# Rope tables made on VectorE a round ahead, first queries turned inside the embedding stage, and a third buffer for x1

## What is computed

```
x = x + L0_ffn(L0_cond(x))          # 16 mixing matrices by sequence, then an int4 weight [512, 512] in fp16
x = x + L1_ffn(L1_cond(x))          # L1_cond: attention with a paged KV cache
x = x + L2_ffn(L2_cond(x))
x = x + L3_ffn(L3_cond(x))

L1_cond: q, k, v = x Wq, x Wk, x Wv     # 32 query heads, 8 key heads of 128
         q, k = rmsnorm(q) * wq, rmsnorm(k) * wk
         q, k = rope(q, pos), rope(k, pos)       # pos = length of the sequence's cache + token
         rope(t) = [t1 cos - t2 sin, t2 cos + t1 sin]
         keys = 512 cached ones (16 pages of 32) and the 32 new ones
         softmax(q keys^T * scale, masked by cache length) values, then Wo
```

## Time and profile before

| what | us |
|---|---|
| median of the three runs | 3247.13 |
| lowest and highest | 3244.84, 3252.37 |
| the profiled execution's own time | 3248.76 |
| its span, first to last instruction | 3246.8 |
| busy in the span: PE, DVE, ACT, POOL | 3034.6 (93%), 1556.9 (48%), 1293.1 (40%), 1532.6 (47%) |
| mean granted clock of TensorE | 0.976 of full |
| DMA | 378.26 MB, mean 117 GB/s |

### The profile page before, as it was taken

How to read it: one execution, slowest core, us unless ns; L and a number is a source line. 1 busy time by engine, 2 the same in 40 slices (tenths; PEclk the granted TensorE clock), 3 DMA queues, 4 the chain that set the end, 5 groups by cost and what they waited for, 6 DMA issues and landing times. The chain is left out here.

```text
span 3246.8 us, 55910 instructions
## 1 busy us (share of the span) xinstructions
PE 3034.6 (93%) x15256; PEld 2022.1 (62%) x15264; DVE 1556.9 (48%) x3931; ACT 1293.1 (40%) x3014; POOL 1532.6 (47%) x1323
## 2 busy tenths in 40 slices
PE   3799999999999999999999999999999986888887
PEld 2466666666666666666666666666666664555454
DVE  6544444444444444444444444444444444556555
ACT  1344444444444444444444444444444431222221
POOL 7355555555555555555555555555555520001000
PEclk9899999999999999999999999999999997999898
DMA  8544444434443444545444444344444443112110
GB/s 294 192 122 123 117 117 117 118 117 118 117 118 117 118 118 125 189 123 176 124 119 120 119 120 121 118 127 123 126 118 123 123 148 100 31 37 53 32 30 13
DMA packets 416196, 378.26 MB, mean 117 GB/s; under 512 B 83427, under 2 KB 347763, under 8 KB 414996
## 3 DMA queue, kind: packets, MB, share of 16 engines
q1 hardware_dynamic: 358484, 186.81, 20.2%
q0 software_dynamic: 50480, 174.40, 17.2%
q10 hardware_dynamic: 7056, 14.46, 1.2%
HBM read 341.23 MB, written 25.85 MB: 113 GB/s over the span
## 5 line engine op out<-in xcount | busy, mean ns | idle before, releaser
L533 DVE CUSTOM_DVE_ANT_0 ps_s<-ps_s,mask 128x544 f32<-128x544 f32 x512 | 374.9, 732 | 938.8 <-PE ps_s L360 929.2
L262 POOL DMA_INDIRECT v_sb<-in_v_rows_w,v_row x504 | 488.3, 969 | 469.3 <-PE ps_oT L385 258.7
L319 PE MATMUL ps_t<-wqkv,xT 128*128 128x512 f32 x1488 | 704.1, 596 | 0.0
L383 PEld LDWEIGHTS ps_oT<-pT,v_sb 128*128 128x128 f32 x4096 | 527.0, 192 | 186.6 <-issue 186.1
L433 ACT ACTIVATE ps_s<-ps_s,nmax 128x544 f32<-128x544 f32 x512 | 352.3, 688 | 628.9 <-DVE nmax L533 627.8
L383 PE MATMUL ps_oT<-pT,v_sb 128*128 128x128 f32 x4096 | 541.3, 275 | 9.8 <-issue 9.8
L343 PE MATMUL ps_t<-wo,oT 128*128 128x512 f32 x1024 | 524.8, 597 | 2.5 <-ACT oT L448 0.9
L359 PE MATMUL ps_s<-k_sb,qT 128*128 128x416 f32 x1024 | 446.9, 518 | 19.2 <-issue 15.2
L543 DVE TENSOR_SCALAR p_sb<-ps_s,rinv 128x544 f32<-128x544 f32 x512 | 401.3, 784 | 23.9 <-DVE rinv L540 0.3
L448 ACT ACTIVATE oT<-ps_oT 128x128 f32<-128x128 f32 x512 | 141.9, 277 | 637.0 <-PE ps_oT L385 634.3
L368 PEld LDWEIGHTS ps_pT<-ident_sb,p_sb 128*128 128x128 f32 x2048 | 251.3, 141 | 188.3 <-issue 185.4
(11 more groups left out here) (216 smaller groups left out, 3775.4 us busy)
## 6 DMA issues: line engine op xcount, KB each, us to landing
k_sb<-in_kT SPq DMA_DIRECT2D x2048, 64.0 KB
v_sb<-in_v_rows_w,v_row POOLq DMA_INDIRECT x512
v_new<-v_raw SPq DMA_DIRECT2D x128, 64.0 KB, 3.3
wo<-in_wo_w POOLq DMA_DIRECT2D x2, 4096.0 KB, 15.3
y_scratch<-y_sb SPq DMA_DIRECT2D x32, 256.0 KB, 2.1
xT<-x1T_scratch POOLq DMA_DIRECT2D x31, 256.0 KB, 4.6
tab<-rope_scratch POOLq DMA_DIRECT2D x31, 256.0 KB, 4.7
wqkv<-in_wqkv_w ACTq DMA_DIRECT2D x6, 1024.0 KB, 10.6
```

The lines of the kernel that those rows point to most:

```text
L262: e.indirect_dma_start(out=v_sb[:, b % 2, c, :], out_offset=None, in_=A["v_rows_w"], in_offset=bass.IndirectOffsetOnAxis(ap=v_row[:, b, c: ...
L319: m = e.matmul(ps_t[bank_of(t)][:, :], xT[:, k, :], wqkv[:, k, 512 * t:512 * t + 512], start=k == 0, stop=k == KC - 1)
L383: e.matmul(ps_oT[:, :], v_sb[:, b % 2, c, h * D:(h + 1) * D], pT[:, u % 2, c, :], start=c == 0, stop=False)
L533: e.tensor_tensor_reduce(out=scores(u), in0=scores(u), in1=mask[:, b % 2, :], scale=-SCALE, scalar=3e38, op0=ALU.add, op1=ALU.min, accum_o ...
```

## The change

The rope tables go to HBM as bare cosines and sines (1 MB, stored once). In each round the load brings 64 KB of them into a buffer csn, and DVE multiplies them with the norm weights in two instructions at unit 1 of the round before the one that uses them (make_tables). For group 0 DVE does this in the embedding stage at g = 2. ACT makes the cosines from the half angles. In the embedding stage DVE begins its angles after two loads, spreads the mixing matrices ahead of the dequantisation, and x1 has three buffers, with the turns two groups behind. The first round's queries and keys are turned and copied inside the embedding stage, through two PSUM banks, three tiles in the last group and two after it; the first key placement and one small exponential stand behind them. The waits for the scratch stores move from the end of the stage to SP's and POOL's programs in the attention stage. Round 0's cache pages are loaded at g = 3 to 10, and two folding sums on DVE move from g = 10 and 12 to 7 and 8. The clearing of v_new moves from DVE to POOL. The page numbers lie on four partitions.

```
-        self.bt = sb("bt", [1, B * NPP], I32)
+        self.bt = sb("bt", [GB, GROUPS * NPP], I32)
...
+        self.csn = sb("csn", [P, 2, D // 2], F32)
+        self.w4 = sb("w4", [P, 4, D], F32)
+        self.qT = sb("qT", [P, 2, HKH, GB, REP, S], F32)
+        self.kT_new = sb("kT_new", [P, HKH, P], F32)
...
+        self.out_x = [sem(f"a_out_x{i}") for i in range(3)]
+        self.out_xT = [sem(f"a_out_xT{i}") for i in range(2)]
+        self.out_fold = sem("a_out_fold")
...
+def make_tables(e, W, cosine, sine):
+
+    for i, t in enumerate((cosine, sine)):
+        part = lambda v: v[:, :, :].rearrange("p (s b) (h n) -> p s b h n", b=2, h=2)[:, :, i, :, :]
+        e.tensor_tensor(part(W.tab), t.unsqueeze(1).unsqueeze(1).broadcast_to([P, 2, 2, D // 2]), part(W.w4), ALU.mult).then_inc(W.tab_made, 1)
...
-    if i == 0 and not (isinstance(r, int) and r == 0):
-        e.wait_ge(W.dma_tab, 16 * r)
-
-        e.wait_ge(W.q_turned, NQT * r)
+    if i == 0:
+        e.wait_ge(W.tab_made, 2 * (r + 1))
+        if not (isinstance(r, int) and r == 0):
+            e.wait_ge(W.q_turned, NQT * r)
...
-                            bt[0:1, bass.ds(g * (GB * NPP) + b * NPP, NPP)], engines=[mybir.EngineType.SP], min_val=0, max_val=PAGES - 1,
+                            bt[b:b + 1, bass.ds(g * NPP, NPP)], engines=[mybir.EngineType.SP], min_val=0, max_val=PAGES - 1,
...
+            e.wait_ge(W.out_fold, 32)
+            for i in range(3):
+                e.wait_ge(W.out_x[i], 16 * len(range(i, GROUPS, 3)))
...
-            def load_x(g):
+            def load_x(g, stored, r):
+
+                for s, n in zip(W.out_xT, stored):
+                    e.wait_ge(s, 16 * n)
+                e.wait_ge(W.tab_made, 2 * r)
                 e.dma_start(xT[:, :, :], x1T_d[bass.ds(g, 1), :, :, :].rearrange("a p k n -> (a p) k n")).then_inc(dma_x, 16)
-                e.dma_start(tab[:, :, :], tab_d[bass.ds(g, 1), :, :, :].rearrange("a p k n -> (a p) k n")).then_inc(dma_tab, 16)
+                e.dma_start(csn[:, :, :], tab_d[bass.ds(g, 1), :, :, :].rearrange("a p k n -> (a p) k n")).then_inc(dma_tab, 16)
...
-                    load_x(xg)
+                    load_x(xg, (GROUPS // 2, GROUPS // 2), r + 2)
...
+            load_x(1, (1, 1), 1)
+            e.memset(v_new[0:P - S, :, :], 0.0).then_inc(v_cleared, 1)
+            e.wait_ge(W.out_fold, 32)
             e.dma_start(wo[:, :, :], A["wo_w"][0]).then_inc(dma_wo[0], 16)
...
-            for t in range(NQT):
-                turn_q(0, t)
...
-            for t in range(NQT):
-                copy_q(0, t, 0)
-            place(0, 0)
...
+            def table(r):
+
+                e.wait_ge(dma_tab, 16 * r)
+                e.wait_ge(rope_step, STEPS * r)
+                make_tables(e, W, csn[:, 0, :], csn[:, 1, :])
...
+                    if u == 1 and not last(r):
+                        table(r + 1)
...
-            e.memset(v_new[0:P - S, :, :], 0.0).then_inc(v_cleared, 1)
...
-    w4 = sb("w4", [P, 4, D], F32)
-    tabs = sb("tabs", [P, GROUPS, 2, D], F32)
+    warm = sb("warm", [P, 1], F32)
...
-    x1 = sb("x1", [P, 2, HID], F32)
+    x1 = sb("x1", [P, 3, HID], F32)
...
-    PAGES_AT = {5: (0, 0), 6: (0, 1), 7: (0, 2), 8: (0, 3), 9: (1, 0), 10: (1, 1), 11: (1, 2), 12: (1, 3)}
-    SUMS_AT = {10: ("w2f", "w2"), 12: ("b2f", "b2")}
+    PAGES_AT = {3: (0, 0), 4: (0, 1), 5: (0, 2), 6: (0, 3), 7: (1, 0), 8: (1, 1), 9: (1, 2), 10: (1, 3)}
+    SUMS_AT = {7: ("w2f", "w2"), 8: ("b2f", "b2")}
...
-            e.wait_ge(out_fold, 32)
-            for i in range(2):
-                e.wait_ge(out_x[i], 16 * (GROUPS // 2))
-                e.wait_ge(out_xT[i], 16 * (GROUPS // 2))
...
-            e.wait_ge(dma_t, 16 * 6)
+            e.wait_ge(dma_t, 16 * 3)
...
-            w4_minus = w4[:].rearrange("p (a b) d -> p a b d", b=2)[:, :, 1, 0:HD]
-            step(e.tensor_scalar(w4_minus, w4_minus, -1.0, None, ALU.mult))
-            e.wait_ge(trig, 2)
-
-            step(e.tensor_tensor(cs, cs, cs, ALU.mult))
-            step(e.tensor_scalar(cs, cs, -2.0, 1.0, ALU.mult, ALU.add))
-
-            def tables(s):
-
-                for h in range(2):
-                    at = slice(h * HD, h * HD + HD)
-                    for i, t in enumerate((cs, sn)):
-                        e.tensor_tensor(tabs[:, :, i, at], t, w4[:, s + i, at].unsqueeze(1).broadcast_to([P, GROUPS, HD]), ALU.mult).then_inc(tab_ready, 1)
-                e.wait_ge(tab_ready, 2 * s + 4)
-                e.dma_start(tab_d[:, :, s:s + 2, :].rearrange("g p k n -> p g (k n)"), tabs[:, :, :, :].rearrange("p g k n -> p g (k n)")).then_inc(out_tab, 16)
-                step(e.tensor_copy(W.tab[:, s:s + 2, :], tabs[:, 0, :, :]))
-
-            tables(0)
             gather(2)
-            e.wait_ge(out_tab, 16)
-            tables(2)
-
-            step(e.tensor_copy(W.v_row[:, :, :], v_rows[:, 0:GB * LC].rearrange("p (b c) -> p b c", b=GB)))
-            e.sem_inc(W.rows_ready, 1)
+            e.wait_ge(trig, 4)
+            e.dma_start(tab_d.rearrange("g p k n -> p k g n"), cs_sn).then_inc(out_tab, 16)
+
+            e.wait_ge(rows_made, 3)
+            e.tensor_copy(W.v_row[:, :, :], v_rows[:, 0:GB * LC].rearrange("p (b c) -> p b c", b=GB)).then_inc(W.rows_ready, 1)
+            e.wait_ge(W.rows_ready, 1)
...
+            e.wait_ge(out_tab, 16)
             rotate(e, W, 0, 0)
             rotate(e, W, 0, 1)
-            e.wait_ge(out_tab, 32)
...
+            def turn_q(t):
+                e.wait_ge(W.rope_step, STEPS1 if t < 3 else STEPS)
+                if t == 0:
+                    e.wait_ge(W.summed, NQT)
+                    e.wait_ge(W.raw_copied, NT)
+                wait(e, W.q_copied, t - 1)
+                for h in range(4):
+                    m = e.transpose(ps_p[t % 2][:, h * P:(h + 1) * P], W.rot[:, 4 * t + h, :], ident[:, :])
+                m.then_inc(W.q_turned, 1)
...
-                if g > 0:
-                    turn(g - 1)
+                if g > 1:
+                    turn(g - 2)
                 if g == FOLD_AT:
                     fold_down()
+                if g == GROUPS - 1:
+                    for t in range(3):
+                        turn_q(t)
+            turn(GROUPS - 2)
             turn(GROUPS - 1)
+            for t in range(3, NQT):
+                turn_q(t)
...
-            for to, of in ((posi[:], "seq_tok"), (invf[:], "inv_freq"), (w4[:], "rope_w"), (btx, "bt_rows"), (voff[:], "row_off"), (seqi, "seq_all")):
+            for to, of in ((posi[:], "seq_tok"), (invf[:], "inv_freq")):
+                e.dma_start(to, A[of]).then_inc(dma_a, 16)
+            e.dma_start(W.w4[:, :, :], A["rope_w"]).then_inc(dma_w4, 16)
+            for to, of in ((btx, "bt_rows"), (voff[:], "row_off"), (seqi, "seq_all")):
                 e.dma_start(to, A[of]).then_inc(dma_t, 16)
...
             e.activation(cs, ang, ACT.Sin, scale=0.5).then_inc(trig, 1)
+            e.wait_ge(trig, 2)
+            e.activation(cs, cs, ACT.Square).then_inc(trig, 1)
+            e.wait_ge(trig, 3)
+            e.activation(cs, cs, ACT.Copy, scale=-2.0, bias=1.0).then_inc(trig, 1)
...
-                    e.wait_ge(rows_made, 1)
+                    e.wait_ge(rows_made, 3)
...
+            def copy_q(t):
+                e.wait_ge(W.q_turned, t + 1)
+                if t < HKH:
+                    to, of = W.qT[:, 0, t, :, :, :].rearrange("p b r s -> p r b s"), ps_p[t % 2][:, :].rearrange("p (r b s) -> p r b s", r=REP, b=GB)
+                else:
+                    to, of = W.kT_new[:, :, :], ps_p[t % 2][:, :].rearrange("p (h n) -> p h n", h=HKH)
+                e.activation(to, of, ACT.Copy).then_inc(W.q_copied, 1)
...
-                    turn_copy(g - 1)
+                if g > 1:
+                    turn_copy(g - 2)
...
+                if g == GROUPS - 1:
+                    for t in range(3):
+                        copy_q(t)
+            turn_copy(GROUPS - 2)
             turn_copy(GROUPS - 1)
+            for t in range(3, NQT):
+                copy_q(t)
+            e.wait_ge(W.q_copied, NQT)
+            e.activation(W.k_sb[:, 0, NPP, :, :], W.kT_new[:, :, 0:S], ACT.Copy).then_inc(W.placed, 1)
+            e.activation(warm[:, :], offs[:, :], ACT.Exp)
...
-            e.wait_ge(dma_t, 16 * 6)
+            e.wait_ge(dma_a, 16 * 2)
...
+            e.wait_ge(bd_zero, 1)
+            spread(0)
             e.wait_ge(dma_q, 16 * 5)
...
-            e.wait_ge(bd_zero, 1)
-            spread(0)
             e.wait_ge(W.dma_bt, 16)
             e.tensor_scalar(W.bt[:, :], W.bt[:, :], 0, PAGES - 1, ALU.max, ALU.min).then_inc(W.bt_bounded, 1)
+            e.wait_ge(dma_w4, 16)
+            minus_sine = W.w4[:, :, :].rearrange("p (s b) d -> p s b d", b=2)[:, :, 1, 0:HD]
+            e.tensor_scalar(minus_sine, minus_sine, -1.0, None, ALU.mult).then_inc(minus, 1)
...
-                wait(e, out_x[i], 16 * (g // 2))
-                wait(e, x1_turned, g - 1)
```

(31 more changed lines are left out.)

25 lines of the change are left out of this document (10 added, 15 removed).

## The result

The changed kernel took 3218.52 us (median of 4 runs, 3216.76 to 3221.14) and the kernel before 3245.99 us (4 runs, 3241.43 to 3252.37): a ratio of 0.9915, 95% interval 0.9896 to 0.9933, so 27.5 us less. Forecast were 3216.0, between 3204 and 3231, and faster. The profiled executions stand at 3217.99 and 3248.76 us, 30.8 us apart, as forecast; what follows asks how much of that is for the forecast's reasons.

The account below looks back on a forecast made before the run. PE's matmuls bound the attention rounds, waits the embedding stage. Gains of 16.4 + 6 + 8.4 = 30.8 us take the profiled 3248.76 to 3218.0, less 1.6 us to the median: 3216, range 3204 to 3231.

Parts of the forecast that it names:

- Start of the products: Embedding stage start: DVE waits for two loads instead of six; ffn(0) at 29.8 instead of 43.6, 14 us earlier.
- POOL's first set: Embedding stage before the change: POOL's first four table products lie over DVE's four small copies, which take 8.08 us.
- To mix(5): Embedding stage, ffn(0) to mix(5): mix(5) at 54.2; together with the start 16.4 us earlier, bounds 12 and 21.
- x late: Rival, embedding stage: x loads come late in full queues, so only 23 us gained, 3224; chance 22%.
- Groups with a projection: Embedding stage, mix(5) to mix(11): PE has no holes, 33.8 us stay, nothing changes.
- The last groups: Mix(11) to end of ffn(15): fewer waits for x, third x1 buffer and later turns gain 6 us, bounds 3 and 8.7.
- The lower bound of 3: Mix(11) to end of ffn(15): only 3 us gained if loads come late again, the same bytes moving in less time.
- ffn(15) to the score: Last ffn to first score: ACT sets it, 8.5 us instead of 16.9; 8.4 us gained, bounds 6 and 10.
- the landing: End of embedding stage: stores' landing, part of the 16.9 us to the first score, is waited for later by SP and POOL.
- POOL: Embedding stage: POOL loses two table sets; its rotation ends at 103.8, hidden with a margin of 3.4 us.
- The rounds: Attention rounds: DVE's two table products, 0.7 us, are covered in unit 1; zero effect, bounds -5 and +5 us.
- The rival of slower, table products held in every round: Rival, unit 1 of each round: one DVE table product held 9.13 us, 7.1 us per round, about 3436; chance 3%.

Follow-up runs that it names:

- a3: Changed kernel with the six projection weight loads issued by SP behind the first x loads instead of by ACT: 3228.67 us, ratio 0.9956.
- c0: The changed kernel itself, unaltered, run and profiled once more: 3216.00 us, ratio 0.992.
- b5: Changed kernel with the old start: DVE's angles wait for all six loads and the first spreading follows the dequantising: 3215.91 us, ratio 0.9924.
- a1: Changed kernel without the small exponential at the end of the embedding stage: 3219.79 us, ratio 0.9931.
- b1: Changed kernel with two x1 buffers instead of three, each turned one group behind instead of two: 3212.00 us, ratio 0.9924.
- b4: Changed kernel with fourteen more products of 128 elements on DVE in unit 1 of every round: 3217.32 us, ratio 0.9923.
- b2: Changed kernel with the first queries' five tiles turned, copied and placed after the embedding stage, as before: 3219.49 us, ratio 0.9936.
- a2: Changed kernel with six buffers for x instead of four: 3211.10 us, ratio 0.9897.
- b3: Changed kernel with the waits for the stores' landing put back at the end of the embedding stage: 3211.07 us, ratio 0.9919.
- a4: Changed kernel with eight unused POOL products put back in two sets of four where the tables had them: 3231.31 us, one run.

## Why the prediction was right

Its sign, its size and nearly all landmarks hold. Point by point:

1. *Start of the products: right, mis-sized by a microsecond.* First product at 19.3 (forecast 19.5), dequantised at 26.85 (27.9), ffn(0) at 31.1 (29.8). The step missed that ACT would be issuing weight loads when its first copy was due; a3 shows it. In c0, with the same code, ffn(0) is at 29.9. The reading of POOL's first set behind this step was loose: it does lie over the copies, but they end at 39.83, 2.2 us before the set does (42.05), so they were not held to its end as the addition was. That they were held b5 shows.
2. *To mix(5): right, on average.* I had x of group 4 at 42.1. In seven executions that leave the start as it is (the first trace, c0, a1 and b1 to b4) mix(4) starts at 41.9 to 45.3: the rival "x late" described the first trace, not c0. The queues are full from 20 to 50 us, at about 400 GB/s, and x of group 4 lands 7.6 us after its issue in c0 and 9.8 in b2. From mix(4) to mix(5) it took 9.3 to 10.4 us, not 12.1: taking 4.58 from the 16.7 of the earlier trace rows left in it what PE's low clock costs behind that hole (the first folding products took 6.31 us before and 4.34 after). The two errors partly cancel.
3. *Groups with a projection: right, for a reason that it doesn't name.* 33.8 us, before and after. With the turns left one group behind it would have been 38.9 (b1), as the first transpose store now lands in full queues.
4. *The last groups: the gain was half, and the reason given for part of it wrong.* 3.1 us in the first trace, 3.2 to 4.1 in the others that leave these groups alone, not 6. The third x1 buffer gives none of it in b1, and in these groups the trace before has only 0.18 us of waiting for x1 to remove. What shrank is the waiting for x, from 5.73 us to 3.74. That the page loads, moved two groups forward, made room for it is likely but untested. The x holes stay (2.14, 1.27 and 0.33 us). The lower bound of 3, "if the loads come late again", is what happened, and a2 shows the rest by taking those waits away.
5. *ffn(15) to the score: right in size* (8.8 us, forecast 8.5) *and in what sets it.* But the landing, which the text counts among what is left behind, was worth nothing with the table load beside it (b3); the five tiles are 7.8 of the 8.1 us (b2).
6. *POOL: right.* The rotation ends at 104.8 (103.8), 3.8 us before the last ffn ends. In a2 it ends at 98.35, behind the last ffn at 95.2, but DVE is later still.
7. *The rounds: right at zero.* Two products take 0.75 us (0.7 forecast), and b4 shows the cover with five times that. All table products in the rounds of the changed kernel, durations in ns (minimum, median, maximum):

```profile
L85 DVE TENSOR_TENSOR tab<-csn,w x62: 415/418/421, 132.2 to 2498.0; 128x256 f32<-128x256 f32 x62
```

The rival of slower, table products held in every round, falls: of 62 products in rounds none is over 421 ns, and of b4's 434 none is over 319. The Trainium skill's rule (SBUF — State Buffer, section "Who interferes with whom") that a two-input DVE instruction can be shut out by GpSimd is borne out in kind by a4's 5.55 us beside POOL's set. It did not speak against the change: around DVE's new products POOL computes nothing and only issues value gathers (four from 1068.91 to 1073.65, beside a pair at 1069.91), and beside those no product is held.

What was forecast at the score is 30.8 us earlier; the first trace has 26.0 and c0, beside the one execution of before, 31.0. So the forecast's sum is as good as one trace can tell. That the profiled executions differ by exactly the forecast 30.8 us is luck: 3.8 of it lie in the spread of the rounds and 1.0 in what follows them.

## What to carry to other kernels

An instruction that another engine holds up costs where its result is next waited for, which can be groups later and on a DMA queue: price the queue behind it. When loads move forward in time, ask which stores then land among them, and who waits for these. Turning tiles one by one between two engines with nothing beside costs the full round trip each, so put them where both have other work. Before making a chain of engines faster, see which load's issue is bound to a buffer that comes free late. Before explaining a few microseconds in a long loop, profile the same kernel twice.

## What the runs showed that was not expected

A hole costs twice. The window of the changed kernel around the end of its largest hole (length, busy times of PE, PEld, DVE, ACT and POOL, granted clock, DMA share, GB/s):

```profile
42.00:48.00 6.00, 2.66 (x10) 2.11 (x11) 0.00 (x0) 0.57 (x1) 3.46 (x4) 0.50 1.04 394
```

After 7.89 us without work PE's granted clock is 0.50, 1.2 GHz. The ffn that follows took 1.91 us instead of 1.03, and from mix(4) to mix(5) it took 10.4 us, where a2, with a hole of 0.96, needed 8.1. (It is no multiple of the hole: 9.3 us after 4.25 in c0, 9.6 after 18.68 in a3.)

The store of the first transpose takes 18.2 us to land in the changed kernel, where the median store takes 3.0; b1 shows what waiting for it costs.

Instruction fetches differ from execution to execution of one kernel (95 and 122), and PE's idle time in the rounds with them. Some of DVE's additions take 1.64 us instead of 0.69 while POOL rotates, in the changed kernel too (two in its last groups). In a2, without the waits for x, they come to the surface.
